# Sliding-window attention's probabilities times values: one fp32 product replaced by three fp16 products of high and low halves

## The reference

```
scores = einsum('bhnqd,bhnkd->bhnqk', qb, kb) / sqrt(d)
p  = softmax(where(mask, scores, -inf), axis=-1)
ob = einsum('bhnqk,bhnkd->bhnqd', p, vb)
...
o_ = 0.5 * y + 0.5 * o_lin
o_ = o_.astype(bfloat16).astype(float32)
o  = o_.transpose(0, 2, 1, 3).reshape(b, n, H * D) @ Wo
```

## Time and profile before

| | |
|---|---|
| median of three runs | 1970.0 us |
| the profiled execution | 1971.56 us |
| its span, first to last instruction | 1969.8 us |
| TensorE busy | 1880.7 us (95%) |
| VectorE busy | 1432.2 us (73%) |
| GpSimd busy | 1266.3 us (64%) |
| ScalarE busy | 1252.7 us (64%) |
| mean granted TensorE clock | 0.985 |

### The profile page before, as it was taken

One profiled execution on the slowest core, in us unless ns is written; L12 is line 12 of the kernel. 1 busy time (PEld: TensorE's weight loads), 2 busy tenths in 40 slices (PEclk: granted clock), 3 DMA queues, 4 the chain that ended last, 5 costly groups with the idle time before them and its releaser, 6 DMA issues. The chain is left out here.

```text
span 1969.8 us, 43595 instructions
## 1 busy us (share of the span) xinstructions
PE 1880.7 (95%) x11700; PEld 1259.0 (64%) x11700; DVE 1432.2 (73%) x3952; ACT 1252.7 (64%) x4898; POOL 1266.3 (64%) x1189
## 2 busy tenths in 40 slices
PE   2899999999999999999999999999999779999997
PEld 2577777677777777776777767777677545444443
DVE  7788888888888888888888888888888664302022
ACT  6577777777777777777777777777777555312121
POOL 4777777777777777777777777777777631212121
PEclk8999999999999999999999999999999989999999
DMA  5000000000000000100000000000000132000000
GB/s 181 28 31 24 24 24 24 29 29 24 24 24 24 24 24 24 32 24 24 24 24 29 24 24 24 24 29 29 24 24 24 68 116 80 23 0 22 0 21 21
DMA packets 47052, 63.87 MB, mean 32 GB/s; under 512 B 5232, under 2 KB 20080, under 8 KB 47024
## 3 DMA queue, kind: packets, MB, share of 16 engines
q1 hardware_dynamic: 47024, 63.52, 10.0%
HBM read 50.86 MB, written 12.65 MB: 32 GB/s over the span
## 5 line engine op out<-in xcount | busy, mean ns | idle before, releaser
L342 POOL TENSOR_TENSOR f_acc<-f_acc,f_s 128x512 f32<-128x512 f32 x416 | 530.8, 1276 | 26.1 <-POOL f_acc L342 0.5
L879 PE MATMUL bank<-wh,xh 128*128 (+1 forms) x1024 | 334.8, 327 | 6.0 <-POOL wl L330 4.2
L879 PE MATMUL bank<-wl,xh 128*128 (+1 forms) x1024 | 334.7, 327 | 0.0
L879 PE MATMUL bank<-wh,xl 128*128 (+1 forms) x1024 | 334.7, 327 | 0.0
L324 POOL TENSOR_TENSOR pr<-pr,rp 128x512 f32<-128x512 f32 x128 | 133.1, 1040 | 210.1 <-DVE rp L616 210.1
L1364 POOL TENSOR_TENSOR hl<-hf,hh 128x512 f16<-128x512 f32 (+1 forms) x44 | 50.8, 1154 | 288.3 <-ACT hh L1233 288.3
L682 DVE TENSOR_SCALAR f_s<-f_nrm 128x512 f32<-128x512 f32 x480 | 227.6, 533 | 4.4
L413 ACT ACTIVATE qe<-bank,nqm 128x128 f32<-128x128 f32 x512 | 180.8, 365 | 78.4 <-DVE qs L547 58.1
L441 ACT ACTIVATE pr<-bank,pmx 128x128 f32<-128x128 f32 x512 | 180.6, 366 | 39.0 <-DVE pmx L609 32.7
L868 PE MATMUL bank<-wh,oT 128*128 (+1 forms) x512 | 194.1, 379 | 2.5 <-ACT oT L482 2.5
L868 PE MATMUL bank<-wl,oT 128*128 (+1 forms) x512 | 194.0, 379 | 0.0
(11 more groups left out here) (181 smaller groups left out, 5150.1 us busy)
## 6 DMA issues: line engine op xcount, KB each, us to landing
raw_qkv<-wq SPq DMA_DIRECT2D x36, 256.0 KB, 2.4
raw_o<-wo SPq DMA_DIRECT2D x36, 256.0 KB, 2.6
f_raw<-wf SPq DMA_DIRECT2D x33, 256.0 KB, 2.7
dequantised<-f_dq SPq DMA_DIRECT2D x32, 256.0 KB, 2.0
wt<-dequantised SPq DMA_DIRECT2D x31, 256.0 KB, 2.9
rows<-x SPq DMA_DIRECT2D x4, 1024.0 KB, 8.6
xr<-x SPq DMA_DIRECT2D x16, 256.0 KB, 4.4
out<-yo SPq DMA_DIRECT2D x16, 256.0 KB, 2.0
```

What stands on the lines that cost most here:

```text
L342: nc.gpsimd.tensor_tensor(f_acc[:], f_acc[:], f_s[:, k % 8, :], ALU.add).then_inc(s["f_ad"], 1)
L879: last = nc.tensor.matmul(dst, av, w[:, sl + c, lo:hi], start=(n == 0), stop=(n == 3 * NC - 1))
```

## The change

The values are scaled on ScalarE to fp32 (`va`, as before) and to an fp16 high half (`vs`, half 0). VectorE makes the low half (`low_v`: values minus high half, 128 x 128, fp16). ScalarE then copies both halves at once from `vs` into the shifted tile `vm` (`shift_v`, two copies of 64 x 256, at the end of its turn). For the probabilities, `copy_pa` writes an fp32 copy and an fp16 high half, both read from the bank X1; GpSimd subtracts them into the low half `pal` (`low_pa`, 128 x 512). The fp32 copy has one buffer instead of two. `output` makes six fp16 matmuls in place of two fp32 ones (high x high, low values x high probabilities, high values x low probabilities, each for `vm` and `vs`) and waits for `pal_p` and `vm_ev`. The linear part's state update (L926) still uses `va` in fp32.

```diff
@@ gpsimd
+            def low_pa(t):
+                wait_tile(pool, s["pa_ev"], t)
+                nc.gpsimd.tensor_tensor(pal[:, t.p % 2, :], pa[:], pah[:, t.p % 2, :], ALU.subtract)\
+                    .then_inc(s["pal_p"], 1)
@@ gpsimd turn
                 if l1.real():
                     softmax_q(l1)
+                if l2.real():
+                    low_pa(l2)
+                if l1.real():
                     nf4_add(l1)
                     softmax_p(l1)
@@ scalar k_exps
                 nc.scalar.activation(va[:, t.p, :], PKV[:, P:2 * P], ACT.Copy, scale=0.5 / WSCALE)
-                nc.scalar.activation(vm[0:WIN, t.p, :], PKV[0:WIN, P:2 * P], ACT.Copy, scale=0.5 / WSCALE)
-                nc.scalar.activation(vm[WIN:P, (t.p + 1) % 4, :], PKV[WIN:P, P:2 * P], ACT.Copy, scale=0.5 / WSCALE)\
+                nc.scalar.activation(vs[:, t.p, 0, :], PKV[:, P:2 * P], ACT.Copy, scale=0.5 / WSCALE)\
                     .then_inc(s["v_ev"], 1)
@@ scalar copy_pa
-                nc.scalar.activation(pa[:, t.p % 2, :], X1[:], ACT.Copy).then_inc(s["pa_ev"], 1)
+                wait_tile(act, s["pal_p"], t, 1)
+                nc.scalar.activation(pa[:], X1[:], ACT.Copy)
+                nc.scalar.activation(pah[:, t.p % 2, :], X1[:], ACT.Copy).then_inc(s["pa_ev"], 1)
+
+            def shift_v(t):
+                wait_tile(act, s["vl_d"], t)
+                nc.scalar.activation(vm[0:WIN, t.p], vs[0:WIN, t.p], ACT.Copy)
+                nc.scalar.activation(vm[WIN:P, (t.p + 1) % 4], vs[WIN:P, t.p], ACT.Copy).then_inc(s["vm_ev"], 1)
@@ scalar turn, at its end
                     copy_ktT(l1)
+                if t.real():
+                    shift_v(t)
@@ vector, in the turn between p_max(l1) and log_decay(t)
+            def low_v(t):
+                wait_tile(dve, s["kabs_ev"], t)
+                nc.vector.scalar_tensor_tensor(out=vs[:, t.p, 1, :], in0=PKV[:, P:2 * P], scalar=0.5 / WSCALE,
+                                               in1=vs[:, t.p, 0, :], op0=ALU.mult, op1=ALU.subtract)\
+                    .then_inc(s["vl_d"], 1)
@@ tensor output
-                wait_tile(pe, s["pa_ev"], t)
-                wait_tile(pe, s["v_ev"], t)
-                for b, v in enumerate((vm, va)):
-                    last = nc.tensor.matmul(PO[:, b * 256:(b + 1) * 256], v[:, t.p, :], pa[:, r, b * 256:(b + 1) * 256],
-                                            start=False, stop=(b == 1))
+                wait_tile(pe, s["pal_p"], t)
+                wait_tile(pe, s["vm_ev"], t)
+                for b, v in enumerate((vm, vs)):
+                    for k, (j, a) in enumerate(((0, pah), (1, pah), (0, pal))):
+                        last = nc.tensor.matmul(PO[:, b * 256:(b + 1) * 256], v[:, t.p, j, :],
+                                                a[:, r, b * 256:(b + 1) * 256], start=False, stop=(b == 1 and k == 2))
```

More of the change, by code:

```diff
@@ L172, in attention @@
         pr = sb("pr", [P, 2, 512])
-        pa = sb("pa", [P, 2, 512])
+        pa = sb("pa", [P, 512])
+        pah = sb("pah", [P, 2, 512], F16)
+        pal = sb("pal", [P, 2, 512], F16)
         oT = sb("oT", [P, 2, GRP, 2, WIN], BF16)
@@ L185, in attention @@
         va = sb("va", [P, 4, P])
-        vm = sb("vm", [P, 4, P])
+        vs = sb("vs", [P, 4, 2, P], F16)
+        vm = sb("vm", [P, 4, 2, P], F16)
         sr = sb("sr", [P, 2, P])
@@ L218, in attention @@
             kmx_d nkm_a kabs_ev kneg_d krope_d g_d gl_d rks_d kt_d qmx_d nqm_a qrope_d rq_d qt_d pmx_d
-            rp_d pm_d pa_ev su_d em_d sr_d acc_d qrope_p krope_p qn_p pn_p
+            rp_d pm_d vl_d vm_ev pal_p pa_ev su_d em_d sr_d acc_d qrope_p krope_p qn_p pn_p
             wqk_sc wqk_hi wqk_lo wo_sc wo_hi wo_lo raw_a raw_b consts z_id
@@ L362, in turn @@
             def turn(t):
-                l1 = t.back(1)
+                l1, l2 = t.back(1), t.back(2)
                 if l1.real():
@@ L379, in _ @@
             pool.wait_ge(s["x_norm"], TILES)
-            turns(pool, 1, turn)
+            turns(pool, 2, turn)
         @block.scalar
@@ L714, in turn @@
                 if t.real():
+                    low_v(t)
                     log_decay(t)
```

## The result

The changed kernel takes 2331.5 us (median of four, 2329.6 to 2335.9) against 1970.1 before: a ratio of 1.184, 95% interval 1.182 to 1.186. It is slower by 361 us. I had said slower, 2219 us, range 2170 to 2275: the side was right, the size was outside the range by 57 us.

What follows compares the result with a forecast made beforehand. TensorE was taken to set three of four turns, VectorE's `kt` turn 1. The profiled 1971.6 us plus 224 for the loop and 25 for the clock gave 2221, less 1.6 for the median: 2219 us, range 2170 to 2275.

Steps and rivals of the forecast that it cites:

- The bound before: TensorE waits for nothing in turns of 11.50 us; turn 1 loses 0.83 us, waiting from VectorE's `kt` onward.
- TensorE, 0.22 us a turn: Output product: six fp16 matmuls take 0.65 us instead of 0.87, cutting a turn to 11.28; alone, 28 us saved.
- the first rival: GpSimd's idle time takes `low_pa` and TensorE goes on setting the pace: faster, 1958 us; chance 0.05.
- The ring through GpSimd, TensorE and ScalarE: GpSimd's wait for `pah` delays its adds, then TensorE's L839, then ScalarE's next `pah`: net 224 us over the program.
- The adds' and VectorE's part in it: GpSimd's adds counted 5.27 us for four, 6.70 for five; VectorE charged only `low_v`, up to 0.29 in turn 1.
- The change, step by step: The prediction's passage costing the change on TensorE, VectorE, ScalarE and GpSimd, ending in a net 224 us added.
- The clock: TensorE falls to 1.2 GHz for 6.83 us behind the 4.0 us gap, once per four turns: 25 us.
- The second rival: TensorE's clock falls also behind the 2.1 us gap at turn 2's end: 2236 to 2258 us; chance 0.15.
- The sum by turns: Turns 0 to 3 take 13.90, 11.28, 13.39 and 15.31 us; turn 0 with a clock fall 14.7.
- that GpSimd's idle time takes the subtraction: GpSimd fits `low_pa` into its idle time, at most 11.05 us of work a turn: 1958 us; chance 0.05.
- That the loop is shorter than read: No clock falls and some link overlaps: 2194 us, or 2171 with 10% less; chance 0.13 for below 2185.

Runs made afterwards that it cites:

- e2: Changed kernel with GpSimd's subtraction and its wait left out, the third product reusing the high half: 1977.0 us, against 1968.5 for the kernel before.
- e4: Changed kernel with VectorE's quantiser compares cut to 64 of 512 columns: 2247.1 us.
- e8: Changed kernel with nine filler transposes on TensorE ahead of the linear scores in turns 3, 0 and 1: 2279.9 us.
- e3: Changed kernel with GpSimd's subtraction on two never-written tiles, so without its wait, the third product reusing the high half: 2021.5 us.
- e11: All three products, the subtraction on VectorE straight from the bank, one GpSimd add moved from turn 3 to turn 0: 1998.7 us, ratio 1.015 to the kernel before.

## Why the prediction was right or wrong

**The bound before** (TensorE in three turns, VectorE's `kt` in turn 1): right; the control with short compares takes 11.50 in all four.

**TensorE, 0.22 us a turn**: right (11.29 in turn 2 of e2, against 11.50 before). Without the ring the prediction's own terms give 1958 us (the first rival), and e2 has 1977. Turn 1 is as it said (12.6); the rest is mostly turn 3, where VectorE takes 0.4 us that the prediction put at nothing.

**The ring through GpSimd, TensorE and ScalarE**: right, as a mechanism and in its links, but for turn 0's adds (5.65 us where I had 5.27, in e4). `nkm` starts 0.32 us after `va` in the changed kernel where I took 0.31, `pah` is 0.59 where I took 0.58. The wait alone makes 246 us, and moving the instruction takes back 282.

**The adds' and VectorE's part in it**: this is the step that failed. In "The change, step by step" VectorE is charged with `low_v` alone, and the compares stand in no term: their price is put at nothing without a reason. I added up what GpSimd's delayed adds do to those who wait for GpSimd, and not what they do to an operation that runs beside them. In turn 2 five compares take 6.33 us instead of 1.88, the scaling of the probabilities and `qtT` are late, and the turn is set by VectorE and not by GpSimd. Short compares take back 84 us. The rows of before had a hint that I did not follow: the compares' line has 533 ns in the mean where one takes 0.42 alone.

**The clock**: the mechanism was right, the size not. I charged 25 us for one fall per four turns, with the low clock for 6.83 us; filling the gaps returns 52. The low clock lasts about as long as that, some 7 us per four turns, but in two pieces, one in turn 3 and one in turn 0 or 1, and each lengthens its turn. The second rival, more falls, was true in part: the gap that VectorE opens at the end of turn 2 is 3.3 us, not the 2.1 I had, and a fall follows it (1.06 at 1020.70). The Trainium skill, "TensorE: Matmul & The Clock Gate", section "HAM oscillation — how this bites in real kernels", has waits in a loop lower the clock again on each pass. The 0.94 over the stage agrees with falls that come back; but they come twice in four turns, and not behind each of the three gaps.

**The sum by turns.** At full clock, in e8, turns 0 to 3 take 14.64, 11.36, 14.78 and 15.58 us, against my 13.90, 11.28, 13.39 and 15.31. That is 2.5 us more per four turns, some 80 us in all; of the 2.5, 1.4 are in turn 2 and 0.7 in turn 0. Half of turn 0's share is its adds. With the 52 of the clock it makes 2194 + 80 + 52 = 2326, against 2331.5 measured. My 14.7 for turn 0 with a fall happens to be its length without one; that is luck.

**The rivals**: that GpSimd's idle time takes the subtraction is refuted by e3 even without the wait, since the idle time was what kept the compares fast. That the loop is shorter than read is refuted by e4, where at full clock it is 0.5 us per four turns longer. More falls are above.

## What to carry to other kernels

Before adding a wait to an engine with a strict order, follow what is queued behind it around to whoever feeds it: if the path comes back, add up the ring and compare it with the turn. Then look at the other engines' timelines for what will newly run beside the shifted work. Where an instruction needs a late input, put it where the input is ready; here that one place was worth 282 us.

## What the runs showed of the hardware

A compare of 128 x 512 fp32 on VectorE takes 0.42 us alone and up to 1.50 while GpSimd works; in a row they then follow each other at GpSimd's pace (five in 6.33 us, beside adds of 1.33). It isn't the amount of data: cut to 64 columns they have a median of 188 ns in the control (mean 278), but a mean of 538 beside the delayed adds (single ones up to 1316), and an operation of 8 columns took 1.1 us in e11. An operation of VectorE with one of its inputs in a bank kept its length in all runs (`qtT`, 675 to 680 ns in the mean, also where GpSimd works beside it). The Trainium skill, "GPSIMD Engine Reference", section 1, says that its SBUF interfaces are shared with VectorE, in contention with instructions in a 2-port mode or with two SBUF inputs. The 8-column operation has two inputs in SBUF and agrees, and so does `qtT`, which has one. The compares read one tensor from SBUF, so by that rule they would have to run in a 2-port mode; the trace doesn't show the mode. By these rows the cost to VectorE is the rest of GpSimd's running instruction, however short VectorE's own is. GpSimd loses little: its adds went from 1276 to 1345 ns in the mean.
